# A deeper attention pipeline with its block steps spread over other slots, other forms for the routing, and hinted loop branches

## What is computed

```python
x = x + layernorm(attention(layernorm(x)))      # 16 heads of 64, causal, keys and values through a 128-wide latent
f = layernorm(x)                                # the rows that are routed
expert = argmax(f @ centroids.T)                # 8 experts
alpha = sigmoid(sum(f * centroids[expert]))
y = f + relu(h(f) @ W1[expert].T + b1[expert]) @ W2[expert].T + b2[expert]    # h: a layernorm with gamma, beta
x = x + layernorm(alpha * y + (1 - alpha) * f)
```

## Time and profile before

| | |
|---|---|
| median of 3 runs | 1459.13 us (1459.09 to 1460.83) |
| profiled execution | 1459.58 us, its span 1457.7 us |
| busy | PE 1343.0 us (92%), DVE 1234.4 (85%), ACT 1083.2 (74%), POOL 809.8 (56%) |
| mean granted TensorE clock | 0.977; in tenths over 40 slices: 9 in 38, 6 and 7 in the two at 1240 and 1440 us |
| first and last t_lo (256 of them) | 17.3 us, 1217.5 us |
| chain that ended last | DVE 46%, issue 22%, ACT 18%, POOL 6%, PE 5% |

### The profile page before, as it was taken

One profiled execution on the slowest core, in us unless ns is written; L12 is line 12 of the kernel. 1 busy time (PEld: TensorE's weight loads), 2 busy tenths in 40 slices (PEclk: granted clock), 3 DMA queues, 4 the chain that ended last, 5 costly groups with the idle time before them and its releaser, 6 DMA issues.

```text
span 1457.7 us, 34718 instructions
## 1 busy us (share of the span) xinstructions
PE 1343.0 (92%) x9120; PEld 1210.6 (83%) x9120; DVE 1234.4 (85%) x4806; ACT 1083.2 (74%) x3186; POOL 809.8 (56%) x1216
## 2 busy tenths in 40 slices
PE   7999999999999999999999999999999999599993
PEld 6988898888888988888888888888888888488872
DVE  5899888888888888888888888888888887499994
ACT  5888787878787878788787878787878886366661
POOL 3445555555555555555555555555555554178886
PEclk9999999999999999999999999999999999699997
DMA  4000000000000000000000000000000000312120
GB/s 194 5 9 12 12 11 12 11 8 11 12 11 12 11 11 10 9 11 11 11 11 12 11 10 11 10 11 12 11 12 11 9 9 14 95 48 63 59 62 8
DMA packets 38793, 32.39 MB, mean 22 GB/s; under 512 B 4882, under 2 KB 35990, under 8 KB 38304
## 3 DMA queue, kind: packets, MB, share of 16 engines
q1 hardware_dynamic: 31968, 21.61, 4.9%
q0 software_dynamic: 4608, 8.67, 1.7%
q10 hardware_dynamic: 2112, 1.11, 0.3%
HBM read 20.35 MB, written 12.07 MB: 22 GB/s over the span
## 4 chain that ended last, share of the span: by engine, by line
DVE 46%; issue 22%; ACT 18%; POOL 6%; PE 5%; ACTq 1%; DMA 1%; DVEq 1%; POOLq 0%; SPq 0%
DVE nscore L851 15%; DVE p_lo L861 13%; ACT prob L722 10%; ACT t_hi L694 5%; DVE nmax L851 2%; POOL prob L1037 2%; DVE ff L367 2%; DVE hitr L891 2%; DVE wup_s L384 1%; DVE on L393 1%; POOL pay L1056 1%; DVE fn L793 1%; DVE gg L402 1%; DVE t_lo L838 1%; DVE rinv L832 1%
## 5 line engine op out<-in xcount | busy, mean ns | idle before, releaser
L1037 POOL TENSOR_TENSOR prob<-prob,rinv 128x256 f32<-128x256 f32 (+1 forms) x512 | 413.2, 828 | 507.8 <-DVE rinv L832 507.7
L722 ACT ACTIVATE prob<-nscore,nmax 128x128 f32<-128x128 f32 (+1 forms) x1024 | 458.7, 449 | 248.4 <-DVE nmax L851 248.4
L851 DVE CUSTOM_DVE_ANT_0 nscore<-psS,mask 128x128 f32<-128x128 f32 (+1 forms) x1024 | 319.9, 350 | 0.0
L861 DVE TENSOR_TENSOR p_lo<-psP,p_hi 128x768 fp32r<-128x768 f32 x256 | 243.7, 952 | 1.0 <-ACT p_hi L694 0.9
L838 DVE TENSOR_TENSOR t_lo<-psT,t_hi 128x512 fp32r<-128x512 f32 x256 | 175.9, 687 | 56.0 <-ACT t_hi L694 56.0
L607 PE MATMUL psP<-ident,prob 128*128 128x128 f32 x1536 | 216.4, 277 | 6.8 <-DVE p_lo L861 6.7
L694 ACT ACTIVATE p_hi<-psP 128x768 fp32r<-128x768 f32 x256 | 204.9, 800 | 1.6 <-PE psP L607 1.6
L579 PE MATMUL psS<-t_lo,xt_hi 128*128 128x256 f32 (+1 forms) x512 | 196.8, 384 | 0.0
L722 ACT ACTIVATION_READ_ACCUMULATOR prob<-nscore,nmax 128x1 f32 x1024 | 191.3, 187 | 0.0
L607 PEld LDWEIGHTS psP<-ident,prob 128*128 128x128 f32 x1536 | 167.2, 141 | 22.7 <-POOL prob L1037 8.8
L867 DVE TENSOR_TENSOR z_lo<-psZU,z_hi 128x512 fp32r<-128x512 f32 x256 | 175.7, 686 | 3.3 <-ACT z_hi L694 3.3
(11 more groups left out here) (167 smaller groups left out, 3246.0 us busy)
## 6 DMA issues: line engine op xcount, KB each, us to landing
fin<-routed_rows SPq DMA_DIRECT2D x40, 136.0 KB, 2.2
wx<-ffn_w SPq DMA_DIRECT2D x2, 2058.0 KB, 12.0
xin<-x SPq DMA_DIRECT2D x32, 128.0 KB, 2.1
xres<-x SPq DMA_DIRECT2D x32, 128.0 KB, 2.1
out<-res,fin POOLq DMA_INDIRECT x80, 2.3
routed_rows<-padr ACTq DMA_DIRECT2D x4, 272.0 KB, 4.3
routed_rows<-padr SPq DMA_DIRECT2D x4, 272.0 KB, 5.4
wup_s<-wup SPq DMA_DIRECT2D x1, 1024.0 KB, 4.9
```

What stands on the lines that cost most here:

```text
L722: last = nc.scalar.activation(prob[:, p1, h, a:z], nscore[:, h, a:z], ACT.Exp, bias=nmax[:, p1, h, q:q + 1], scale=-1.0, accum_out=rsum[:, ...
L851: last = v.tensor_tensor_reduce(nscore[:, h, a:z], psQ[q][:, h, :], mask[:, a:z], -1.0, -MASKED, ALU.add, ALU.min, nmax[:, p1, h, q:q + 1])
L861: v.tensor_tensor(p_lo[:, (s - 3) % 2], psP[:, :, 0:384], p_hi[:, (s - 3) % 2].bitcast(F32), ALU.subtract).then_inc(S["p_split"], 1)
L1037: last = g.tensor_tensor(pr, pr, rinv[:, p2, :, q:q + 1].broadcast_to([P, 2, z - a]), ALU.mult)
```

## The change

- The pipeline of a pair gets one slot more. ScalarE takes the exponentials for q = 1 a slot later, ahead of the q = 0 ones (and nscore has two buffers for it); P, Z and U come a slot later.
- On VectorE the slot is now: early block steps (`misc_early`), t_lo, nscore q = 0, p_lo, nscore q = 1, rinv, late block steps (`misc_late`), z_lo.
- Block steps have other slots. TensorE turns xn in r = 1 (was 5), fn in r = 3 (was 2), and scores and ranks in r = 4 and 5 (were 3 and 4). GpSimd computes rs2 in r = 0 behind its product (was r = 7), the sum x1 in r = 1 (was 0), and the scatter in r = 7 (was 5). `an` is a late step of r = 0, the statistics of the sum one of r = 1.
- xn and fn are normalised on GpSimd (were VectorE's), and x is loaded one block earlier.
- Routing: hits and hitr are one form with a scalar (`scalar_tensor_tensor`, once for each half), the one-hot is two `tensor_scalar`, dsum goes to PSUM.
- The spare rows of `routed_rows` are stored from GpSimd's queue (was SP's); the wait for stored rows is in r = 3 (was 7).
- The two loops of every engine carry a hint for the branch back.

The core of the diff:

```diff
+        def hinted_loop(eng, first, end):
+            return nc.Fori(first, end, engines=bass.OrderedEngineSet([eng.engine]), hint_back_edge=True)
...
-                with eng.Fori(1, ITERS - 1) as it:
+                with hinted_loop(eng, 1, ITERS - 1) as it:
...
-                if live(3):
-
-                    p3 = (s - 3) % 4
-                    pe.wait_ge(S["norm_ready"], g0 + s - 2)
-                    if live(4):
-                        pe.wait_ge(S["p_split"], g0 + s - 3)
+                if live(4):
+
+                    pe.wait_ge(S["norm_ready"], g0 + s - 3)
+                    if live(5):
+                        pe.wait_ge(S["p_split"], g0 + s - 4)
                     for h in range(2):
                         for k in range(3):
                             last = nc.tensor.transpose(psP[:, h, k * P:(k + 1) * P],
...
-                if live(4):
-
-                    zb, zx = (s - 4) % 2, ((s - 4) // PAIRS) % 2
-                    pe.wait_ge(S["p_split"], g0 + s - 3)
-                    if (s - 4) % PAIRS == 0:
-                        pe.wait_ge(S["xk_split"], b0 + (s - 4) // PAIRS + 1)
-                    if live(5):
-                        pe.wait_ge(S["z_split"], g0 + s - 4)
+                if live(5):
+
+                    zb, zx = (s - 5) % 2, ((s - 5) // PAIRS) % 2
+                    pe.wait_ge(S["p_split"], g0 + s - 4)
+                    if (s - 5) % PAIRS == 0:
+                        pe.wait_ge(S["xk_split"], b0 + (s - 5) // PAIRS + 1)
+                    if live(6):
+                        pe.wait_ge(S["z_split"], g0 + s - 5)
...
-                if live(5):
-
-                    ub, ur = (s - 5) % 2, (s - 5) % PAIRS
...
+                if live(6):
+
+                    ub, ur = (s - 6) % 2, (s - 6) % PAIRS
...
+                if r == 1 and live_b(-1):
+                    pe.wait_ge(S["xn_ready"], b0 + db + 2)
+                    if live_b(2):
+                        pe.wait_ge(S["a_norm"], b0 + db - 1)
+                    turn_x()
+                if r == 3 and live_b(2):
                     pe.wait_ge(S["f_ready"], b0 + db - 1)
+                    if live_b(-1):
+                        pe.wait_ge(S["x_split"], b0 + db + 2)
+                    else:
+                        pe.wait_ge(S["a_norm"], b0 + db - 1)
...
+                if live(2):
+                    exps(1, 2)
                 if live(1):
-                    exps(0)
-                if live(4):
-                    act.wait_ge(S["z_ready"], g0 + s - 3)
-                    if live(6):
-                        act.wait_ge(S["u_done"], g0 + s - 5)
-                    cp(z_hi[:, (s - 4) % 2], psZ[:]).then_inc(S["z_hi_done"], 1)
-                if live(1):
-                    exps(1)
+                    exps(0, 1)
+                if live(5):
+                    act.wait_ge(S["z_ready"], g0 + s - 4)
+                    if live(7):
+                        act.wait_ge(S["u_done"], g0 + s - 6)
+                    cp(z_hi[:, (s - 5) % 2], psZ[:]).then_inc(S["z_hi_done"], 1)
...
-                misc(g0, b0, s, live, live_b)
+                misc_early(g0, b0, s, live, live_b)
                 route(b0, s, live_b, 0)
+                if live(0):
+                    dve.wait_ge(S["t_hi_done"], g0 + s + 1)
+                    v.tensor_tensor(t_lo[:, s % 2], psT[:], t_hi[:, s % 2].bitcast(F32),
+                                    ALU.subtract).then_inc(S["t_split"], 1)
+                route(b0, s, live_b, 1)
+
...
+                route(b0, s, live_b, 2)
+                if live(4):
+                    dve.wait_ge(S["p_hi_done"], g0 + s - 3)
+                    v.tensor_tensor(p_lo[:, s % 2], psP[:, :, 0:384], p_hi[:, s % 2].bitcast(F32),
+                                    ALU.subtract).then_inc(S["p_split"], 1)
+                route(b0, s, live_b, 3)
+                if live(1):
+                    score_max(1)
+                route(b0, s, live_b, 4)
                 if live(2):
                     p2 = (s - 2) % 4
                     dve.wait_ge(S["probs_ready"], 2 * (g0 + s - 1))
                     v.reciprocal(rinv[:, p2].rearrange("p h q -> p (h q)"),
...
+                misc_late(g0, b0, s, live, live_b)
+                if live(5):
+                    dve.wait_ge(S["z_hi_done"], g0 + s - 4)
+                    v.tensor_tensor(z_lo[:, (s - 5) % 2], psZ[:], z_hi[:, (s - 5) % 2].bitcast(F32),
                                     ALU.subtract).then_inc(S["z_split"], 1)
...
-                        dve.wait_ge(S["argmax_steps"], 4 * n + 1)
-                        v.tensor_tensor(hits[:], scv, over(best), ALU.is_ge).then_inc(S["argmax_steps"], 1)
+                        dve.wait_ge(S["argmax_steps"], 3 * n + 1)
+                        for t in range(2):
+                            last = v.scalar_tensor_tensor(hitr[:, t, :], scv[:, t, :], best[:, t:t + 1], rev_e[:],
+                                                          ALU.is_ge, ALU.mult)
+                        last.then_inc(S["argmax_steps"], 1)
                     elif k == 2:
-                        dve.wait_ge(S["argmax_steps"], 4 * n + 2)
...
+                        dve.wait_ge(S["argmax_steps"], 3 * n + 3)
+                        for t in range(2):
+                            last = v.tensor_scalar(oh[:, t, :], rev_e[:], first[:, t:t + 1], None, ALU.is_equal)
+                        last.then_inc(S["onehot_ready"], 1)
...
-                        v.tensor_tensor(dsum[:], scv, base[:, db, :].unsqueeze(1).broadcast_to([P, 2, E]), ALU.add)
+                        v.tensor_tensor(dsv, scv, base[:, db, :].unsqueeze(1).broadcast_to([P, 2, E]), ALU.add)
...
+            def misc_early(g0, b0, s, live, live_b):
...
-                    aggregate(st1, mv1, S["st1_done"], S["mv1_done"], b0 + db + 2)
+                    prep_turned((db + 1) % 2, b0 + db + 2)
+                if r == 3 and live_b(-2):
+                    dve.wait_ge(S["xn_ready"], b0 + db + 2)
+                    prep_stats(db, b0 + db + 3)
...
+                if r == 4 and live_b(2):
+
+                    n = b0 + db - 1
+                    dve.wait_ge(S["r3_steps"], 6 * n - 4)
+                    v.scalar_tensor_tensor(pay[:, db, :, C_SHIFT], mv3[:, :, 0], -1.0, pay[:, db, :, C_RSTD],
...
+            def misc_late(g0, b0, s, live, live_b):
...
+                if r == 3 and live_b(-2):
+                    aggregate(st1, mv1, S["st1_done"], S["mv1_done"], b0 + db + 3)
...
+            def prep_rstd(n):
+                inv_sqrt(rs1[:], ve1, mv1[:, :, 1], S["mv1_done"], S["ve1_done"], S["rs1_done"], n)
+
+            def prep_norm(par, n):
+
+                wait_apart(pool, S["rs1_done"], n)
+                pool.wait_ge(S["xk_split"], n - 1)
+                normalise(lambda t: xn[:, t, :], lambda t: xin[:, par, t, :], mv1,
+                          lambda t: rs1[:, t:t + 1], S["xn_ready"])
 
...
                 if r == 0 and live_b(2):
+                    inv_sqrt(rs2[:], ve2, mv2[:, :, 1], S["mv2_done"], S["ve2_done"], S["rs2_done"], b0 + db - 1)
+                if r == 1 and live_b(2):
                     n = b0 + db - 1
                     pool.wait_ge(S["a_norm"], n)
                     pool.wait_ge(S["xr_loaded"], 16 * n)
                     g.tensor_tensor(pay[:, db, :, 0:P], an[:], xres[:, db], ALU.add).then_inc(S["x1_ready"], 1)
-                if r == 1 and live_b(2):
...
+                if r == 2 and live_b(2):
                     n = b0 + db - 2
...
+                    g.tensor_tensor(rs3, ve3[:], neg_half[:], ALU.pow).then_inc(S["r3_steps"], 1)
+                    wait_apart(pool, S["r3_steps"], 6 * n + 2)
+                    normalise(lambda t: fn[:, t, :], lambda t: pay[:, db, t, 0:P], mv3,
+                              lambda t: pay[:, db, t, C_RSTD:C_RSTD + 1], S["f_ready"])
+                if r == 3 and live_b(2):
+                    pool.wait_ge(S["rows_written"], 16 + 32 * (b0 + db - 2))
...
+                if r == 4 and live_b(-2):
+                    prep_rstd(b0 + db + 3)
...
+                if r == 5 and live_b(-1):
...
+                if r == 6 and live_b(-2):
+                    prep_norm(db, b0 + db + 3)
+                if r == 7 and live_b(2):
...
-                if r == 7 and live_b(1):
-                    inv_sqrt(rs2[:], ve2, mv2[:, :, 1], S["mv2_done"], S["ve2_done"], S["rs2_done"], b0 + db)
```

More of the change, by code:

```diff
@@ L110, in block_kernel @@
         rinv = sb("rinv", [P, 4, 2, 2])
-        nscore = sb("nscore", [P, 2, 384])
+        nscore = sb("nscore", [P, 2, 2, 384])
         prob = sb("prob", [P, 4, 2, 384])
@@ L129, in block_kernel @@
         ft = sb("ft", [P, T])
-        hits = sb("hits", [P, 2, E])
         hitr = sb("hitr", [P, 2, E])
@@ L209, in ffn_phases @@
                 slot(0, 0, s, lambda lag: s >= lag)
-            with eng.Fori(1, TILES // FU) as it:
+            with hinted_loop(eng, 1, TILES // FU) as it:
                 m0 = eng.snap(it * FU)
@@ L664, in slot @@
```

(43 more changed lines are left out.)

194 lines of the change are left out of this document (60 added, 134 removed).

## The result

The changed kernel takes 1533.16 us (median of 4 runs, 1532.67 to 1535.62) against 1459.11 (4 runs): a ratio of 1.0509, 95% interval 1.0491 to 1.0527. It is 74 us slower, inside the predicted range and 34 us above the predicted 1499.

What follows compares the result with a forecast made beforehand. It took a loop over VectorE and ScalarE to set the 4.31 us slot, TensorE close behind. Stalls +63, edges -25.5, first slots -1.5, drain +4 make +40 on 1459.6: 1499 us against the median, range 1476 to 1542.

Steps and rivals of the forecast that it cites:

- The mechanism: GpSimd's rs2, x1 and fn queue behind a product waiting for late rinv, delaying VectorE and TensorE: 2.1 us more a block.
- The plain slot: From one t_lo to the next in an ordinary slot: 4.31 us falls to 4.21, TensorE's floor.
- the edge's stop: VectorE's 2.26 us stop at an iteration's start: hinted back edges save 13 x 1.96 = 25.5 us.
- the one-hot's wait: TensorE's 1.10 us wait in the routing slot goes, with new forms and the one-hot asked for a slot behind the scores.
- the three stalls: TensorE waits 1.85 us at Z of slot 1, 1.72 at Z of slot 2 and 0.5 for fn, each block.
- The stall at fn: TensorE waits for fn, normalised on GpSimd behind product and root: 0.5 us a block (0.3 to 0.8).
- TensorE's floor: TensorE's block without stalls: 8 x 4.21 us plus 1.3 for block steps, 35.0 us.
- The drain: Behind the last t_lo, one slot more and the two waits against short slots: +4 us (0 to +8).
- The first 16 slots: Start of the attention loop, 0.10 us saved a slot: -1.5 us.
- Waits hidden: Rival: rs2 and x1 are ready in time or z_lo has slack, a block costs its floor: 1377 us; chance 14%.
- The hint does nothing: Rival: the edge stays in full, +25.5 us, 1525 us; chance 15%.
- The clock falls: Rival: stalls bring TensorE 1.2 in place of 2.4 GHz for 3 us a block, +45 us, 1544 us; chance 8%.

Runs made afterwards that it cites:

- the fastest version: The changed kernel with GpSimd's small steps (rs2, x1, root and fn) and the two scatters of r = 7 ahead of its product: 1367.65 us, ratio 0.9367.
- the two runs on the hint: The changed kernel without the hint on its branches back: 1555.42 us; the kernel before with that hint alone: 1434.91 us.

## Why the prediction was right, and where its sizes were off

**The mechanism held at each step.** an waits 2.68 (foreseen about 2.7), the statistics 2.43 (2.3), TensorE at Z 1.78 and 1.55 (1.85 and 1.72), and taking the three steps out from behind the product takes 146 us off. The plain slot is 4.18 (4.21), the edge's stop is gone with 22 to 26 us (25.5), the one-hot's wait too. (4.18 is the median of r = 7, the one slot of the changed kernel's block without block steps on TensorE or a stall near it.) Without stalls TensorE's block is 69.73 / 2 = 34.86 us in the fastest version (35.0).

**That the time fell in the range was in part luck.** The forecast by itself was 1476 to 1522, the three stalls each 0.25 off. 1533 lies outside it; it is inside 1476 to 1542 because the upper end had been set for a hint that fails, and the hint did not fail. The iteration of 80.2 us was even named as the sign of that rival (78 for the forecast). The missing "issue" row and the two runs on the hint decide against it; the 2 us are stalls that were priced too low.

**Three terms were too small,** by 34 us in sum. The 15 iterations behind the first 16 slots made 67.5 us where the terms gave 63 - 25.5 = 37.5:

- *The stall at fn, 0.5 us.* It is 1.26, 0.76 more, 23 us over 30 blocks. The pair's form was priced near the cast (one input, 0.6 for the pair, and 0.9 as the upper end); it takes 1.58, twice 0.79, about the time of GpSimd's two-input sum (0.74) for half as many elements. The bound was too low, not only the choice. And the two sizes are joined: with x1 in time the same pair costs 0.5.
- *TensorE's floor added to bare stalls.* The block is 40.12 us; less 4.6 of shown waits that leaves 35.5, not the 34.86 of a block without stalls. Each of the three stalls thus costs about 0.2 more than its idle row, 0.66 a block, 20 us. Against it the stalls at Z were 0.24 a block smaller than foreseen and the floor 0.14 lower, together -11. A matmul's end is modelled, so the rows can't say where the 0.2 lies. The sum, 23 + 20 - 11 = 32, is close to the 30 found (67.5 - 37.5).
- *The drain, +4 (0 to +8).* It is +11. Two terms were left out: at its block's start the root stands behind the scatters of r = 7 as well as the product (an waits 3.48 there, 0.80 more than in the loop, and TensorE 4.13), and late steps have little beside them to be hidden by. With small steps and scatters ahead of the product the stretch is 242.0 us instead of 251.1, so 9 of the 11 belong to that order. Part of it may be the clock: behind the last t_lo the granted clock is at 0.50 for 41 us of the next 65, for 31 before and for 27 in that fastest version. No run separates what this costs. Timeline of TensorE and of VectorE in the drain:

```profile
1291.18 0.47 PE L628 MATMUL psZU<-p_hi,xk_lo 128*128 128x512 f32 x1 [4.13 <-DVE z_lo L863]
```

```profile
1289.71 0.73 DVE L796 TENSOR_SCALAR an<-psM,mv,rs 128x128 f32<-128x128 f32 x2 [3.48 <-POOL rs L977]
```

The first 16 slots gave 5.5 us rather than 1.5. From the t_lo of slot 2 to that of slot 7 there are 22.2 us before and 17.0 with the change, where 0.10 a slot was foreseen. As the first t_lo starts 0.6 later, 3.4 of the 4.0 count. Together 30 - 3.4 + 7 = 34.

**A right term with a wrong reason.** "The new forms read one SBUF tensor", so the routing would not stand beside GpSimd's product. The wait did go, but the one-hot's tensor_scalar, one SBUF tensor and a scalar per partition, takes 0.22 us alone and up to 0.88 while the product runs. In the changed kernel it is short because rinv, and with it the product, comes later; with rinv earlier the wait of 1.3 us was back. The Trainium skill (GPSIMD Engine Reference, Specifications, the row on SBUF interfaces) names VectorE instructions in a 2-port mode beside those with two SBUF inputs as the ones that contend with GpSimd. The prediction used only the second half; the one-hot's 0.88 agrees with the first, though no run here shows in which mode it ran.

**The rivals.** *Waits hidden* (1377) did not come by itself, but its sum comes near the two versions with GpSimd's steps ahead: 1387 and 1368. *The hint does nothing* (1525) is refuted on both kernels. *The clock falls* (1544), at a price of 3 us at half speed in each block, is refuted for the changed kernel: the mean grant is 1.00 from 400 to 800 us, with stalls of 1.8. But it is not that such stalls never bring a lower grant. Between the first 16 slots and the last t_lo there were two falls, each back within 4 us and each behind a wait of 1.8 us. TensorE's row and the clock of the first (columns as above):

```profile
1010.96 0.47 PE L628 MATMUL psZU<-p_hi,xk_lo 128*128 128x512 f32 x1 [1.79 <-DVE z_lo L863]
```

```profile
1014.00:1016.00 2.00, 2.00 (x12) 2.00 (x12) 0.11 (x1) 0.78 (x2) 1.85 (x3) 0.53 0.00 0
```

Without the hint it happened much more often, see below.

## What to carry to other kernels

A step in an engine's queue is as late as the latest thing ahead of it: before moving a small step to another slot, look at what stands ahead of it there and when that can start, and put steps whose inputs are long ready ahead of the one that waits. An engine can head the critical path at 59% busy. And a change of several parts can hold good ones (here 49 us) under a rest that costs more (122 us), and of that rest the order of a few lines in one queue decides the sign: with these lines in another place the whole change is 93 us faster than the kernel before.
